# A graph network of two layers on one core: the second layer's mask is written into PSUM by ScalarE, and the work lists are set in another order

## What is computed

```python
# layer 0
q, k = heads(src @ Wq + bq), heads(src @ Wk + bk)
attn = softmax(q k^T / sqrt(32))
out = sum over r of (attn * (adj == r)) @ heads(src @ Wv[r] + bv[r])
x = layernorm(src + out @ Wo + bo)
x = layernorm(x + gelu(x @ W1 + b1) @ W2 + b2)
# layer 1
q, k, v = heads(x @ Wq), heads(x @ Wk), heads(x @ Wv)
e = q k^T
e = where(e >= 0, e, 0.2 * e)
attn = softmax(where(adj > 0, e, -9e15))
h = layernorm(attn @ v)
y = layernorm(concat(h, x) @ Wffn.T) + x
```

## Time and profile before

| | |
|---|---|
| median of three executions | 3339.44 us |
| the profiled execution | 3334.01 us |
| its span, first to last instruction | 3332.2 us |
| TensorE busy | 3145.0 us, 94% |
| VectorE busy | 2796.8 us, 84% |
| ScalarE busy | 2096.9 us, 63% |
| GpSimd busy | 1472.3 us, 44% |
| mean granted TensorE clock | 0.989 |

### The profile page before, as it was taken

One profiled execution on the slowest core, in us unless ns is written; L12 is line 12 of the kernel. 1 busy time (PEld: TensorE's weight loads), 2 busy tenths in 40 slices (PEclk: granted clock), 3 DMA queues, 4 the chain that ended last, 5 costly groups with the idle time before them and its releaser, 6 DMA issues.

```text
span 3332.2 us, 77396 instructions
## 1 busy us (share of the span) xinstructions
PE 3145.0 (94%) x28930; PEld 2717.6 (82%) x28930; DVE 2796.8 (84%) x4892; ACT 2096.9 (63%) x4300; POOL 1472.3 (44%) x1549
## 2 busy tenths in 40 slices
PE   2899999999999999999999999999999999999996
PEld 1788888888888888888888888888888888888885
DVE  3688888888888888888888888888888888888885
ACT  1456666667667667666666666666666667666664
POOL 0344444444444444444444444444444444444441
PEclk8999999999999999999999999999999999999997
DMA  3333433333333333333433433433433333333331
GB/s 104 80 77 87 105 78 85 104 79 85 103 80 85 102 81 85 104 79 85 105 78 85 106 78 85 105 78 85 104 79 85 104 79 85 103 81 85 103 74 33
DMA packets 217643, 292.63 MB, mean 88 GB/s; under 512 B 31492, under 2 KB 119048, under 8 KB 217608
## 3 DMA queue, kind: packets, MB, share of 16 engines
q1 hardware_dynamic: 217608, 292.16, 34.1%
HBM read 72.89 MB, written 16.78 MB: 27 GB/s over the span
## 4 chain that ended last, share of the span: by engine, by line
PE 64%; SPq 8%; POOL 6%; DVE 6%; DMA 6%; ACT 4%; issue 4%; POOLq 0%; DVEq 0%; ACTq 0%
PE pair L914 33%; PE pair L944 11%; SPq L303 7%; PE pair L968 5%; DMA stack_a<-qk 5%; POOL probs L402 4%; PE pair L1027 3%; PE pair L959 3%; DVE n L680 3%; PE pair L960 3%; ACT probs L523 2%; POOL rstd L392 2%; PE pair L919 2%; PE pair L932 1%; PE pair L1036 1%
## 5 line engine op out<-in xcount | busy, mean ns | idle before, releaser
L396 POOL TENSOR_TENSOR act_r_lo<-act,act_r_hi 128x512 fp32r<-128x512 f32 x256 | 343.5, 1345 | 659.1 <-DVE act_r_hi L759 522.3
L496 ACT ACTIVATE leaky_s<-pair 128x1024 f32<-128x1024 f32 x256 | 260.4, 1028 | 436.9 <-PE pair L960 436.9
L502 ACT ACTIVATE leaky_s<-leaky_s,low_r 128x256 f32<-128x256 f32 x1024 | 506.7, 496 | 10.2 <-DVE low_r L722 3.5
L726 DVE TENSOR_REDUCE mx_a<-pair 128x4 f32<-128x1024 f32 x256 | 306.3, 1216 | 105.7 <-PE pair L1027 105.6
L402 POOL TENSOR_TENSOR probs<-probs,rel 128x512 f32<-128x512 f32 x256 | 309.4, 1229 | 164.0 <-ACT probs L523 164.0
L390 POOL TENSOR_TENSOR rstd<-mv,eps 128x2 f32<-128x2 f32 x256 | 72.2, 282 | 652.9 <-DVE mv L669 652.9
L523 ACT ACTIVATE probs<-pair 128x1024 f32<-128x1024 f32 x256 | 263.1, 1028 | 127.8 <-PE pair L1036 125.4
L718 DVE TENSOR_TENSOR leaky_s<-pair,leaky_s 128x1024 f32<-128x1024 f32 x256 | 306.5, 1218 | 5.5 <-ACT leaky_s L496 5.5
L492 ACT ACTIVATE probs<-pair 128x1024 f32<-128x1024 f32 x256 | 260.3, 1018 | 77.8 <-PE pair L968 73.6
L722 DVE TENSOR_REDUCE low_r<-leaky_s 128x4 f32<-128x1024 f32 x256 | 303.8, 1208 | 0.0
L402 POOL TENSOR_TENSOR leaky_s<-probs,rel 128x512 f32<-128x512 f32 x256 | 300.9, 1205 | 0.0
(11 more groups left out here) (180 smaller groups left out, 9113.0 us busy)
## 6 DMA issues: line engine op xcount, KB each, us to landing
stack_a<-qk SPq DMA_DIRECT2D x768, 128.0 KB, 2.9
stack_r<-qk SPq DMA_DIRECT2D x768, 128.0 KB, 2.4
xt<-in_xT SPq DMA_DIRECT2D x64, 256.0 KB, 3.2
adj_a<-in_adjT SPq DMA_DIRECT2D x64, 256.0 KB, 3.1
xn<-in_x SPq DMA_DIRECT2D x64, 256.0 KB, 3.0
adj_q<-in_adj SPq DMA_DIRECT2D x64, 256.0 KB, 2.9
out<-n SPq DMA_DIRECT2D x64, 256.0 KB, 2.2
probs<-in_w SPq DMA_DIRECT2D x4, 512.0 KB, 3.2
```

The source lines that it names most:

```text
L396: return nc.gpsimd.tensor_tensor(dst, src, hi, ALU.subtract)
L502: last = nc.scalar.activation(leaky_s[:, p % SLOTS, k, t], leaky_s[:, p % SLOTS, k, t], ACT.Exp, bias=low_r[:, p, k, t:t + 1], accum_out=d ...
L726: return nc.vector.tensor_reduce(mx_a[:, :, p * NG:(p + 1) * NG].rearrange("p t h -> p h t"), pair[b][:], AX.X, ALU.max)
```

## The change

The second layer's mask isn't added by products any more. ScalarE writes it into both banks of the pair (`masks`, one instruction for each pair of heads, signal `masks_done`), and the score products are added onto it (`start=False`). All four pairs of heads use banks 6 and 7 for this (`B_RR` all 3), and nothing else uses these banks; the other work is placed on banks 0 to 5. Two products with `start=True` open the two banks once, ahead of the first turn. 16 mask products a graph are gone, and 4 ScalarE instructions a graph are new. All five lists are in another order. Of what moved, this is what the next sections speak of:

- TensorE: `masked_rows(0)` stands directly behind `lk`, ahead of `one(0)` and `one(1)`, and `masked_rows(1)` first in the next turn; `lv` stands between `vee(1)` and `masked_rows(3)`; `up(3)` waits for `ashift`.
- ScalarE: `masks` of a pair stands behind the wait for `leaky` of the pair before.
- SP: `stack_r` in two halves with the loads of `xn` and `adj_q` between, then all of `stack_a` behind both parts of `qk_split`, later `xt`, the store and `adj_a`.
- GpSimd: `xt_lo` and the four `masked` stand first in the turn.
- VectorE: `rel1` waits for GpSimd's products and stands behind `lowest_row(0)`, the count of known entries opens the next turn ahead of `att`.

```diff
-        B_AO, B_ADEN, B_Q, B_K, B_WO, B_X1T, B_RV, B_HN = 2, 4, 3, 7, 4, 6, 3, 4
-        B_DN, B_N1T, B_FFN, B_AMT, B_X2T, B_LQ, B_LK, B_LV = 3, 3, 0, 7, 5, 3, 6, 1
+        B_AO, B_ADEN, B_Q, B_K, B_WO, B_X1T, B_RV, B_HN = 2, 4, 0, 5, 3, 4, 0, 5
+        B_DN, B_N1T, B_FFN, B_AMT, B_X2T, B_LQ, B_LK, B_LV = 3, 3, 5, 2, 3, 1, 3, 1
         B_X = 0
-        B_V, B_UP = (5, 4), (7, 1, 3, 2)
-        B_RR, B_TN, B_AR, B_AC = (2, 3, 0, 2), (1, 0, 2, 1), (0, 3, 2, 3), (3, 1, 3, 3)
+        B_V, B_UP = (4, 5), (4, 5, 3, 2)
+        B_RR, B_TN, B_AR, B_AC = (3, 3, 3, 3), (1, 1, 0, 0), (1, 0, 1, 0), (0, 2, 0, 0)
...
+            def masks(b):
+                return copy(pair[b][:], off_q[:].unsqueeze(1).broadcast_to([P, 2, NT, N]))
...
                         dst = pair[b][:, k, t]
-                        mm(dst, stack_r[:, 0, slot(h), t * P:(t + 1) * P], stack_r[:, 1, slot(h), :], start=True, stop=False)
-                        last = mm(dst, identb[:], off_q[:, t, :], start=False, stop=True)
+                        last = mm(dst, stack_r[:, 0, slot(h), t * P:(t + 1) * P], stack_r[:, 1, slot(h), :], start=False, stop=True,
+                                  skip_group_check=True)
...
+            for h in range(2):
+                last = mm(pair[B_RR[0]][:, h].rearrange("p t n -> p (t n)"), onesr[:], bias_r[:, 0:2 * D], start=True, stop=True)
+            last.then_inc(seeds_open, 1)
```

More of the change, by code:

```diff
@@ L335, in body @@
                         load_x_terms(g2)
[L336 to L340, removed]
-                if g3 is not None:
[L342 to L346, removed]
+                if g3 is not None:
+                    load(xt, xT, g3, "(t p) n -> p t n", ld_xt)
                 if g0 is not None:
@@ L350, in body @@
                 if g3 is not None:
[L351 to L355, removed]
+                    load(adj_a, adjT, g3, "(t p) n -> p t n", ld_adj_a)
             turns(sp, body)
@@ L561, in body @@
                     gelu(2, B_UP[2]).then_inc(act_done.sem, 1)
+                if g0 is not None:
+                    act_e.wait_ge(pvr_mm.sem, pvr_mm.at(g0))
+                    copy(att[:], bank(B_RV)).then_inc(att_r_done.sem, 1)
+                if g1 is not None:
                     act_e.wait_ge(act_split.sem, act_split.at(g1, 1))
@@ new lines, in body @@
+                if g2 is not None and not path.general:
+                    nc.vector.tensor_tensor(lowest[:], lowest[:], known[:], ALU.min).then_inc(lowest_done.sem, 1)
+                if g0 is not None:
+                    dve.wait_ge(exp_r_done.sem, exp_r_done.at(g0))
+                    nc.vector.reciprocal(rden_r[:], den_r[:]).then_inc(rden_done.sem, 1)
+                if g2 is not None:
+                    dve.wait_ge(amt_mm.sem, amt_mm.at(g2))
+                    shift(bank(B_AMT)[0:H, 0, :], shift_a, g2, ashift_hi, ashift)
@@ L1085, in body @@
                     projection("wq", (xt_hi, xt_lo), B_Q).then_inc(q_mm.sem, 1)
+                    projection("wk", (xt_hi, xt_lo), B_K).then_inc(q_mm.sem, 1)
                 if g2 is not None:
                     pe.wait_ge(att_split.sem, att_split.at(g2))
-                    if ran(g2, 1):
-                        pe.wait_ge(leaky_done.sem, leaky_done.at(g2 - 1, 1))
                     out_projection(B_WO).then_inc(wo_mm.sem, 1)
+                if g1 is not None:
+                    pe.wait_ge(masks_done.sem, masks_done.at(g1, 3))
+                    pe.wait_ge(stacked_r[2].sem, stacked_r[2].at(g1))
+                    masked_rows(2, B_RR[2]).then_inc(sr_mm.sem, 1)
@@ L1091, in body @@
                 if g3 is not None:
                     vee(0, B_V[0]).then_inc(v_mm.sem, 1)
-                    if ran(g3, 1):
-                        pe.wait_ge(res_a_done.sem, res_a_done.at(g3 - 1))
-                    vee(1, B_V[1]).then_inc(v_mm.sem, 1)
-                    projection("wk", (xt_hi, xt_lo), B_K).then_inc(q_mm.sem, 1)
+                if g1 is not None:
+                    if ran(g1, -1):
+                        pe.wait_ge(res_a_done.sem, res_a_done.at(g1 + 1))
+                    turn(0, B_TN[0]).then_inc(turned_mm.sem, 1)
```

546 lines of the change are left out of this document (280 added, 266 removed).

## The result

The changed kernel takes 3645.49 us (median of four executions, 3643.26 to 3647.70); the kernel before took 3338.6 beside it. The ratio is 1.092, interval 1.090 to 1.093. The profiled execution has a span of 3643.7 us, and a mean granted clock of 0.935 where it was 0.989. The forecast was 3710, the range 3490 to 3870.

A forecast was written before the change was run, and what follows sets the result against it. TensorE's issue was taken as the bound: 45.0 us plus 9.3 of waits and 1.5 for the clock, 55.8 a turn against 50.0. Over 63 turns +365, ends +5, on 3334.0: 3704, as median 3710 us, range 3490 to 3870.

The forecast's parts named there:

- The 45.0 us of issue: TensorE's time to issue one turn's products and transposes in the changed kernel, without waits: 45.0 us.
- The first wait: TensorE, behind `lk`: `masked_rows(0)` waits for the `stack_r` DMA, 5.2 to 5.8 us a turn, taken as 5.5.
- Two bare chains: Ways from `lk` or SP's `stack_r` to the scores in the last and first turns, giving 5.2 and 5.8 us.
- The second and third wait: TensorE waits 1.7 us a turn ahead of `masked_rows(1)` and 0.8 ahead of `out_proj`.
- 1.5 us for the clock: TensorE's products behind the first wait run partly at 1.2 GHz: 1.5 us a turn, range nothing to 4.
- The middle: Waits later in the turn: `score_rows(1)` 0.6 us, three others 0.3 together, up(3) 0.4.
- The walk's 54.3: Turn length from following all engines' lists: 45.0 us of issue plus 9.3 of waits, before the clock term.
- Rival 1: Waits as counted with the clock high, or the middle hidden: 52.2 to 54.5 us a turn, 3480 to 3625; chance 0.20.
- Rival 3: Landing of `stack_r` hidden, all waits of a turn under 5.0: 49.0 us a turn, 3275 us; chance 0.05.
- Rival 4: Only the first wait counts: 50.2 us a turn, no measurable difference; chance 0.03.
- Rival 2: ScalarE and GpSimd fall behind: 58 to 60 us a turn, 3850 to 3970 us; chance 0.14.
- The second theory: Formed after x3 to x7: a loop from `lk` through `stack_a` to `score_rows(1)` and back sets the turn, 54.9 us.

The follow-up runs named there:

- x1: Changed kernel's order and banks, with the mask products back on TensorE and ScalarE's masks gone: 3753.86 us, 56.7 us a turn.
- x2: Changed kernel with neither kind of mask, so the second layer attends to all nodes: 3635.39 us, 54.8 us a turn.
- x5: Changed kernel plus 36 products that nobody reads, between `lk` and `masked_rows(0)`: 3617.93 us, 54.5 us a turn.
- x3: Changed kernel with score products of pairs 0 and 1 reading a weight tile, so not waiting for `stack_r`: 3618.42 us, 54.6 us a turn.
- x4: Changed kernel with one(0) moved ahead of `masked_rows(0)`: 3731.85 us, 56.3 us a turn.
- x10: x8 with VectorE splitting `lk` ahead of the result's scaling and SP sending `stack_r` ahead of the store: 3676.71 us, 55.4 us a turn.
- x11: x10 with the two edits of x9: 3647.63 us, 55.0 us a turn.
- x8: Changed kernel with both(1) moved behind `lk`, and the transposes of `x2` and their two parts earlier: 3669.32 us, 55.3 us a turn.
- x12: x11 with two of GpSimd's eight mask products made earlier, while it waits for statistics: 3716.70 us, 56.1 us a turn.
- x9: Changed kernel with `lv` right behind `lk`, and VectorE making the first-layer keys' low part before the residual add: 3624.72 us, 54.6 us a turn.
- x7: Changed kernel with the next turn's `wq` and `wk` moved between `lk` and `masked_rows(0)`: 3736.85 us, 56.3 us a turn.

## Why the prediction was right

**What bounds it, and the products.** The products were put at 2.0 us a turn and gave 1.9 (x1 to x2). The 45.0 us of issue were too few. The same 45 middle turns by windows, of the changed kernel and of x5:

```profile
598.36:3070.42 2472.06, 2212.11 (x19621) 1881.08 (x19620) 1940.19 (x3422) 1604.92 (x3196) 1001.14 (x1080) 0.94 0.34 81
```

```profile
598.61:3048.92 2450.31, 2323.89 (x21241) 2023.86 (x21240) 1940.09 (x3422) 1607.96 (x3196) 1003.90 (x1080) 0.99 0.34 82
```

In x5, near full clock, TensorE is busy 51.6 us a turn and idle 2.8. 4.2 of the busy time are the issue of the 36 products without a reader, so its work takes 47.4 us, and 7.0 would be waiting. The prediction had 45.0 and 9.3 for the same. So the issue was some 2.4 us too low and the waits 2.3 too high, and as far as these runs show it is luck that the two meet. The kernel before has the first of the two errors as well: in its middle TensorE is idle for 1.2 us a turn, where the prediction had 3.0 of waits. In the changed kernel 49.2 us a turn are busy and 5.8 idle; the 1.8 us of work beyond 47.4 are the slow stretch, most of it in the place of waiting.

**The masks.** Forecast 1.03 each, 1.023 came, between the neighbours of the earlier trace rows and nearest to PSUM to SBUF. That their share costs nothing and only their place might: x2 puts both together at 0.1 us a turn.

**The first wait.** Forecast 5.5 behind `lk`, came 5.48, and 335.6 us in all for the 350 named. Two bare chains at the ends of the run held for all 64 graphs. The landing of the third DMA took 2.49 us in the turn shown; with the 2 of the Trainium skill the first wait would have come out half a microsecond short. The Trainium skill, DMA: Bandwidth & Descriptors, has that figure in the section Anatomy of one DMA — SWDGE (gpsimd) path, and not in the section that the prediction names; it is a fit for DMAs that GpSimd issues, and these are issued by SP.

**The second and third wait.** `masked_rows(1)` was put at 9.5 and stands at 10.2, `out_proj` at 13.7 and stands at 13.85; GpSimd's products at 8.1, they end at 7.55. But TensorE isn't idle for 1.7 and 0.8 there: one(0) and one(1) took 1.7 and 1.9 us, not 0.9 each, and filled the time. The table of waits has 22.6 us for all masks together, 0.35 a turn. This is the step that failed: in the sum I had the waits as idle time and then 1.5 us for the clock on top. The slow products ran inside the second wait, as the prediction says of part of them, and so cost nothing there. What remains of the clock is the 0.7 us by which the slow `masked_rows(0)` delays the chain; x5 measures 0.5. The term should have been 0.5, not 1.5.

**The middle.** `score_rows(1)` 0.6 and up(3) 0.4 were forecast; the trace has 0.25 to 0.4 for each. Of what was to show the forecast right, the turn (54 to 57), the mean clock (under 0.97; 0.935), ScalarE's share (64%; 63%) and the 350 us came; the 1.5 us ahead of `masked_rows(1)` did not. The walk's 54.3, with 0.5 for the clock, gives 54.8 where 54.9 came, by errors of opposite sign, as the first paragraph has it.

**The sum.** The turns added 290.5 us where 365 was forecast. Of the 75 between them 63 are the clock's microsecond too many, and most of the rest is that the first turns are shorter than 54.9. The ends grew by 21 and not 5: what fills and drains isn't the same as before the change, since `lk`, `masked_rows` and the masks of the last graphs stand bare. The two errors partly cancel, and the sum, 3704 against profiled runs, is 58 us too high, of an increase of 311; the 5.4 added for the median makes the rest of the difference to 3645.

**The rivals.** Rival 1 (the clock stays high, 52.2 to 54.5) missed the turn by little at its upper end, and its time, up to 3625, by 20 us. It was nearer than the forecast in this term: the clock did fall, but was worth only 0.5 us a turn. Rival 3 (faster, the landing hidden) was named with the point from which it decides, all waits of a turn under 5.0; they were 6.0 and the landing was not hidden. Rival 4 had 50.2 a turn and falls by the 54.9; x3 shows why, since without the landing the turn hardly moves. Rival 2 needs ScalarE or GpSimd behind; they are not in the changed kernel, but GpSimd is in x3, x4, x10 and x11, as soon as TensorE comes to it earlier.

**What the prediction did not see.** It takes "the first wait decides" as the cause, and x3 refutes that: take the wait away and 27 of 307 us come back. It walked along all lists and so came near the time, but put the price on one row of the walk, though other ways were about as long. The second theory made the same error once more, which x8 and x10 to x12 show.

## What to carry to other kernels

When work is taken off the busiest engine by giving up buffers, price the new order and banks apart from the work: here the products gave back 118 us, order and banks together took 415. In a kernel whose engines work fixed lists, a wait's length isn't what its removal brings; walk the ways that don't touch the waiting engine first, and see by how much they are shorter. The chain of waits shows only the longest. A test is to move a step on another engine by half a microsecond and see whether the turn follows; compare turns of the same granted clock then, since in x9 the turn followed only where the clock was higher.

## What was not expected of the hardware

**A VectorE instruction beside GpSimd's products takes two and a half times as long.** The scaling by `rstd` (128x256, both inputs in SBUF) takes 480 ns where GpSimd is idle and 1223 ns beside its products, the row of `n<-n,rstd,x2k` at the top. Of these 128 instructions of the changed kernel, the 124 that overlap a GpSimd instruction of over 0.6 us took 985 to 1392 ns, the 4 others 476 to 485. In x12 the scalings of `x2` lie beside GpSimd's products too (126 of 128, 789 to 1374 ns), and the mean of all 256 of `x` rises. The changed kernel, then x12, groups by line:

```profile
L692 DVE SCALAR_TENSOR_TENSOR x<-x,rstd,norm 128x256 f32<-128x256 f32 x256 | 112.2, 480 | 2.8 <-POOL rstd L386 0.5
```

```profile
L694 DVE SCALAR_TENSOR_TENSOR x<-x,rstd,norm 128x256 f32<-128x256 f32 x256 | 189.2, 779 | 2.8 <-POOL rstd L386 0.5
```

77 us more, if the 128 took it all, is 0.60 each. The new lists also swapped who meets GpSimd: `n<-n,rstd,norm`, further up VectorE's list, had 1254 ns in the kernel before and has 483 now, `n<-n,rstd,x2k` had 481. The Trainium skill, SBUF — State Buffer, section SBUF: two separate sides, states that VectorE with two inputs in SBUF and GpSimd hold a common pair of ports one instruction at a time; that fits, since 0.74 us more is less than one GpSimd product (1.15 to 1.24 us), which such an instruction may have to sit out.

**The clock falls and hardly matters, or matters more than the wait.** Behind the first wait the four score products took 1.15 us from start to start, at full clock 0.48 (0.12 each), and the 16 value products 1.71 where they take 0.9. Two stretches of the same turn by windows, behind the wait and 0.5 us later:

```profile
1726.00:1731.00 5.00, 4.82 (x37) 2.41 (x37) 2.47 (x3) 2.05 (x2) 2.25 (x3) 0.50 0.93 243
1731.50:1736.50 5.00, 4.94 (x41) 4.60 (x40) 4.04 (x8) 4.43 (x13) 2.69 (x3) 1.00 0.28 61
```

The granted clock is 0.50, 1.2 GHz, in the first of them and 1.00 in the second, and a turn loses 0.5 us by it (x5), since most of those products lie where the mask is waited for anyway. In x4 and x7, with several waits in place of the long one, the same work took 1.6 and 1.3 us a turn longer. In x4 the slow stretch reaches into `wq`, `wk` and `out_proj`, which don't stand in the place of a wait. TensorE is idle in x4 for no longer than in the changed kernel (459 us of the span and 474), at 0.902 and 0.935 of the clock: what the clock costs hangs on which work lies in the slow stretch. In the range of the prediction, nothing to 4 us, the trace stands near the lower end. The upper part, which by the prediction would hold by the rule of the Trainium skill (TensorE: Matmul & The Clock Gate, section Loop structure matters more than you think), did not come.
